# A four-layer graph network on one core: order of the prologue's loads, and where a scratch memory is cleared

## What is computed

```
edge_feat = concat([x[src], x[dst], edge_attr]); h = mish(edge_feat @ W1 + b1)
messages  = mish(h @ W2 + b2)
agg       = segment_sum(messages, dst)
u         = mish(concat([x, agg]) @ W3 + b3); y = x + u @ W4 + b4
x         = layernorm(x + (layernorm(y) * gamma + beta))
```

## Time and profile before

| | us |
|---|---|
| median of 3 runs | 1333.28 (1331.62 to 1339.01) |
| the profiled execution's own time | 1331.4 |
| its span | 1329.7 |
| PE busy in the span | 1249.7 (94%) |
| mean granted PE clock | 0.973 of full speed |
| start to last matmul of Z | 90.7 |
| first matmul of the edge phase | 96.9 |
| first matmul of block 1 | 110.9 |

### The profile page before, as it was taken

The page is one execution under the profiler, slowest core; times in us unless marked ns, Lnnn a source line. Parts: engine busy times, 40 slices in busy tenths (PEclk is TensorE's granted clock), DMA queues, the critical chain, the costliest instruction groups (busy, mean ns, idle before and its releaser), DMA issues. The chain is left out here.

```text
span 1329.7 us, 18809 instructions
## 1 busy us (share of the span) xinstructions
PE 1249.7 (94%) x5868; PEld 1000.0 (75%) x5868; DVE 1034.8 (78%) x1815; ACT 854.3 (64%) x775; POOL 665.9 (50%) x484
## 2 busy tenths in 40 slices
PE   6987999999999999999999999688799997999998
PEld 5766777777777777777777777467587775888886
DVE  3435999999999999999999999866776247847444
ACT  3307999999999999999999999437633011212210
POOL 0137688888878887888887886153230000011000
PEclk8998999999999999999999999889999997999999
DMA  9968777777777777777777777269200520000001
GB/s 308 329 213 175 155 148 153 155 152 157 152 148 146 151 156 153 153 154 156 157 151 144 148 157 175 57 231 348 99 2 0 202 66 15 17 1 2 1 20 59
DMA packets 105386, 178.34 MB, mean 134 GB/s; under 512 B 34786, under 2 KB 44304, under 8 KB 105320
## 3 DMA queue, kind: packets, MB, share of 16 engines
q0 software_dynamic: 71056, 106.45, 41.3%
q1 hardware_dynamic: 27176, 58.85, 12.8%
q10 hardware_dynamic: 7088, 12.20, 2.7%
HBM read 139.11 MB, written 38.15 MB: 133 GB/s over the span
## 5 line engine op out<-in xcount | busy, mean ns | idle before, releaser
L213 POOL DMA_INDIRECT w_raw<-q_dram,idx_all x172 | 332.8, 1935 | 73.3 <-issue 56.0
L932 PE MATMUL ps_x<-wA_hi,hT_hi 128*128 128x512 f32 x668 | 270.4, 405 | 1.3 <-DVE hT_lo L701 1.3
L932 PE MATMUL ps_x<-wA_hi,hT_lo 128*128 128x512 f32 x668 | 264.4, 396 | 0.0
L932 PE MATMUL ps_x<-wA_lo,hT_hi 128*128 128x512 f32 x668 | 264.1, 395 | 0.0
L213 POOL DMA_INDIRECT w_raw<-p_dram,idx_all x176 | 176.7, 1004 | 149.5 <-issue 106.3
L932 PEld LDWEIGHTS ps_x<-wA_hi,hT_hi 128*128 128x128 f32 x668 | 125.6, 188 | 34.1 <-issue 1.7
L932 PEld LDWEIGHTS ps_x<-wA_hi,hT_lo 128*128 128x128 f32 x668 | 125.5, 188 | 30.1
L932 PEld LDWEIGHTS ps_x<-wA_lo,hT_hi 128*128 128x128 f32 x668 | 125.5, 188 | 28.5
L708 DVE TENSOR_TENSOR x<-ps_x,b 128x512 f32<-128x512 f32 x167 | 113.7, 681 | 26.5 <-PE ps_x L932 24.4
L1602 POOL TENSOR_TENSOR tmp_n<-X,gam 128x512 f32<-128x512 f32 x10 | 13.9, 1393 | 225.6 <-DVE t_be L1687 180.8
L892 PE MATMUL ps_x<-ident,w_raw 128*128 128x128 f32 x672 | 103.4, 277 | 13.9 <-DVE h L694 7.6
(11 more groups left out here) (280 smaller groups left out, 2894.2 us busy)
## 6 DMA issues: line engine op xcount, KB each, us to landing
ea_raw<-in_eaT SPq DMA_DIRECT2D x88, 128.0 KB, 4.4
adj_dram<-adj_sb POOLq DMA_DIRECT2D x42, 210.2 KB, 9.7
adj_dram<-b ACTq DMA_DIRECT2D x11, 640.5 KB, 5.4
U_lo<-adj_dram SPq DMA_DIRECT2D x10, 640.0 KB, 8.1
adjT_dram<-adjT_sb SPq DMA_DIRECT2D x10, 640.0 KB, 7.4
w_raw<-in_w SPq DMA_DIRECT2D x5, 1024.0 KB, 8.1
adjT_rest<-adjT_dram SPq DMA_DIRECT2D x7, 640.0 KB, 9.9
w_raw_g<-in_w SPq DMA_DIRECT2D x4, 1024.0 KB, 7.7
```

The source lines that it names most:

```text
L213: g.indirect_dma_start(G[:, slot, c * D:(c + 1) * D], None, rows, bass.IndirectOffsetOnAxis(ap=idx_all[:, i:i + 1], axis=0), **op).then_in ...
L932: last = t.matmul(ps_x2[c % 2][:, :], h[:, b.slot, e], w[:, k, :], start=(k == 0 and i == 0), stop=(k == KD - 1 and i == 2))
```

## The change

In words, by engine:

- **ACT, loads:** `w0b` (1024 KB) is issued after the casts of `w0a` and of X1, no longer right behind `w0a`. Its casts move from tiles 1 to 4 to tiles 6 to 9 (DVE's matching subtractions too).
- **SP, loads:** W2 and `wc_raw` are issued behind the store of P0; the biases behind the store of P3; the first edge attributes behind the stores of Q0 and Q1.
- **ACT, clearing:** no pair stands in P. Pairs 0 to 3 alternate with the casts of W3; pair k waits until product R+2k+2 is out (`m_out`), and from pair 5 on the wait is `2R+1`, the first Z product. So pairs 5 to 10 are issued in one row from there.
- **SP, end:** Z's stores count on a semaphore that outlives the stage (`z0_out`). The stage's end no longer waits for their landing. `o_sb` shares memory with the edge phase's `x2` (its second half), so DVE waits for `z0_out` before it first writes there (block 1), and SP before it loads Z back in the first layer's stage.

```diff
-CLEAR_FROM = 1
+        z0_out = sem("z0_out")
+            x2 = sb("x2", [P, 2, TE * D], F32, edges)
-        o_sb = sb("o_sb", [P, OUTS, D], F32, ctx)
+        o_sb = x2[:, 1, :].rearrange("p (u d) -> p u d", u=OUTS)
...
-                sp.dma_start(w2_raw[:, :, :], by_slices(w02)).then_inc(w2_in, 16)
-                for half in range(2):
-                    sp.dma_start(wc_raw[half * ED:(half + 1) * ED, :], w0c).then_inc(w2_in, 16)
-                sp.dma_start(b1[:, :], bcast(b01)).then_inc(b_in, 16)
-                sp.dma_start(b2[:, :], bcast(b02)).then_inc(b2_in, 16)
-                sp.dma_start(b3[:, :], bcast(b03)).then_inc(b3_in, 16)
-                for b in range(2):
-                    load_edge_attr(sp, ea_raw, eaT, b, b, ea_in[b])
                 for r in range(R):
                     sp.wait_ge(p_evac, r + 1)
                     store(p_dram, r, r, st_out[r % OUTS])
+                    if r == 0:
+                        sp.dma_start(w2_raw[:, :, :], by_slices(w02)).then_inc(w2_in, 16)
+                        for half in range(2):
+                            sp.dma_start(wc_raw[half * ED:(half + 1) * ED, :], w0c).then_inc(w2_in, 16)
+                    if r == 3:
+                        sp.dma_start(b1[:, :], bcast(b01)).then_inc(b_in, 16)
+                        sp.dma_start(b2[:, :], bcast(b02)).then_inc(b2_in, 16)
+                        sp.dma_start(b3[:, :], bcast(b03)).then_inc(b3_in, 16)
...
                     store(q_dram, r, m, st_out[m % OUTS])
+                    if r < 2:
+                        load_edge_attr(sp, ea_raw, eaT, r, r, ea_in[r])
                 for r in range(ZM, R):
                     sp.wait_ge(z_evac, r - ZM + 1)
-                    store(z0_dram, r - ZM, 2 * R + r - ZM, z_out)
+                    store(z0_dram, r - ZM, 2 * R + r - ZM, z0_out)
...
-                sp.wait_ge(z_out, 16 * (R - ZM))
...
-                    if 2 <= r < 2 + KD:
-                        low(KD + r - 2)
+                    if r >= R - KD:
+                        low(2 * KD + r - R)
...
-                act.dma_start(w_raw[:, KD:, :], by_slices(w0b)).then_inc(w_in[KD], 16)
                 x_high(0)
                 for k in range(KD):
                     high(k)
-                act.wait_ge(z_ready, 1)
+                x_high(1)
+                act.dma_start(w_raw[:, KD:, :], by_slices(w0b)).then_inc(w_in[KD], 16)
                 for r in range(R):
...
-                    if 1 <= r < 1 + KD:
-                        high(KD + r - 1)
+                    if r >= R - KD:
+                        high(2 * KD + r - R)
...
-                    if r >= CLEAR_FROM:
-                        clear(r - CLEAR_FROM)
-                for r in range(R - CLEAR_FROM, DROWS // P):
-                    act.wait_ge(m_out, R + r - R + CLEAR_FROM + 1)
-                    act.sem_inc(turn, 1)
-                    clear(r)
+                act.wait_ge(z_ready, 1)
                 act.wait_ge(w3_in, 16)
                 act.wait_ge(m_out, R)
                 act.sem_inc(turn, 1)
                 for k in range(KD):
                     a.copy(w_hi[:, k, :], w2_raw[:, k, :]).then_inc(w3_hi, 1)
+                    act.wait_ge(m_out, R + 2 * k + 2)
+                    act.sem_inc(turn, 1)
+                    clear(k)
+                for r in range(KD, DROWS // P):
+                    act.wait_ge(m_out, min(R + 2 * r + 2, 2 * R + 1))
+                    act.sem_inc(turn, 1)
+                    clear(r)
...
+                        if c == 0 and b.it2 is None and b.k == 1:
+                            dve_.wait_ge(z0_out, 16 * (R - ZM))
                         dve_.wait_ge(x2_ready, b.count(TE, c + 1))
...
                     if s == 0:
+                        sp.wait_ge(z0_out, 16 * (R - ZM))
```

More of the change, by code:

```diff
@@ L192, in gnn @@
                     X, w_raw, b4, wA_hi, wA_lo, wc_hi, wc_lo, b2, b3, x, src, dst, w0a, w0b, w0c, b01, w02, b02, w03, b03,
-                    p_dram, q_dram, z0_dram, agg_dram, adj_dram, zero_out, p_in, q_in, eaT, ea_raw, ea_in)
+                    p_dram, q_dram, z0_dram, agg_dram, adj_dram, zero_out, p_in, q_in, eaT, ea_raw, ea_in, x2, z0_out)
             edge_phase(nc, sb, pb, sem, edge_sem, prep_sems, ident, half_pi, relT, srcT, qT, idx_all, base_f, base_i, npass, iota_src,
                        X, Y, w_raw, b3, b4, gam, bet, wA_hi, wA_lo, wc_hi, wc_lo, b2, p_dram, q_dram, agg_dram, adj_dram, eaT, w03,
-                       w04, b04, g0, be0, w3b_in, w4_in, vec_in, zero_out, p_in, q_in, ea_raw, ea_in)
+                       w04, b04, g0, be0, w3b_in, w4_in, vec_in, zero_out, p_in, q_in, ea_raw, ea_in, x2, z0_out)
         Y += [sb(f"Y{r}", [P, D]) for r in range(ZE, R)]
@@ L203, in gnn @@
         first_layer(nc, sb, pb, sem, edge_sems, ident, half_pi, eps_col, X, U_hi, U_lo, Y, w_raw, w_hi, w_lo, b3, b4, gam, bet, deg, rdeg, nrdeg, has, slow,
-                    agg_dram, adj_dram, adjT_dram, z0_dram, w1l, b1l, w1r, w3b_in, w4_in, vec_in, adjT_held, adj_held)
+                    agg_dram, adj_dram, adjT_dram, z0_dram, w1l, b1l, w1r, w3b_in, w4_in, vec_in, adjT_held, adj_held, z0_out)
         edge_numbers.close()
@@ L223, in prepare @@
             X, w_raw, zeros, w2_hi, w2_lo, wc_hi, wc_lo, b2, b3, x, src, dst, w0a, w0b, w0c, b01, w02, b02, w03, b03,
-            p_dram, q_dram, z0_dram, agg_dram, adj_dram, zero_out, p_in, q_in, eaT, ea_raw, ea_in):
+            p_dram, q_dram, z0_dram, agg_dram, adj_dram, zero_out, p_in, q_in, eaT, ea_raw, ea_in, x2, z0_out):
     with ExitStack() as ctx:
@@ L244, in prepare @@
         (z_ready, ident_ready, b_in, b2_in, b3_in, idx_in, pad_set, dve, w_hi_ready, w_lo_ready, idx_tr, idx_ready, t_ready, hi_ready,
-         lo_ready, m_out, p_evac, q_evac, z_evac, w2_in, w2_split, w2_low, w3_in, w3_hi, w3_lo, z_out, turn) = [
+         lo_ready, m_out, p_evac, q_evac, z_evac, w2_in, w2_split, w2_low, w3_in, w3_hi, w3_lo, turn) = [
             prep_sem("prep_" + n) for n in (
@@ L248, in prepare @@
                 "idx_ready", "t_ready", "hi_ready", "lo_ready", "m_out", "p_evac", "q_evac", "z_evac", "w2_in", "w2_split",
-                "w2_low", "w3_in", "w3_hi", "w3_lo", "z_out", "turn")]
+                "w2_low", "w3_in", "w3_hi", "w3_lo", "turn")]
         w_in = [prep_sem(f"prep_w_in{k}") for k in range(KD + 1)]
@@ L441, in _ @@
                     high(k)
-                act.wait_ge(z_ready, 1)
+                x_high(1)
+                act.dma_start(w_raw[:, KD:, :], by_slices(w0b)).then_inc(w_in[KD], 16)
                 for r in range(R):
-                    if r + 1 < R:
+                    if 1 <= r and r + 1 < R:
                         x_high(r + 1)
-                    if 1 <= r < 1 + KD:
-                        high(KD + r - 1)
+                    if r >= R - KD:
+                        high(2 * KD + r - R)
                     if 1 + KD <= r < 1 + 2 * KD:
@@ L524, in edge_phase @@
                X, Z, w_raw, b3, b4, gam, bet, w2_hi, w2_lo, wc_hi, wc_lo, b2, p_dram, q_dram, agg_dram, adj_dram, eaT, w03,
-               w04, b04, g0, be0, w3b_in, w4_in, vec_in, zero_out, p_in, q_in, ea_raw, ea_in):
+               w04, b04, g0, be0, w3b_in, w4_in, vec_in, zero_out, p_in, q_in, ea_raw, ea_in, x2, z0_out):
     HB = 2 * BE
@@ L538, in edge_phase @@
         hT_lo = sb("hT_lo", [P, 2, KD * BE], F32R, ctx)
-        x2 = sb("x2", [P, 2, TE * D], F32, ctx)
         m2 = sb("m2", [P, 2, TE * D], F32, ctx)
@@ L998, in first_layer @@
 def first_layer(nc, sb, pb, sem, sems_to_clear, ident, half_pi, eps_col, X, U_hi, U_lo, Z, w_raw, w_hi, w_lo, b3, b4, gam, bet, deg, rdeg, nrdeg, has, slow,
-                agg_dram, adj_dram, adjT_dram, z0_dram, w1l, b1l, w1r, w3b_in, w4_in, vec_in, adjT_held, adj_held):
+                agg_dram, adj_dram, adjT_dram, z0_dram, w1l, b1l, w1r, w3b_in, w4_in, vec_in, adjT_held, adj_held, z0_out):
     with ExitStack() as ctx:
```

## The result

The change makes the kernel slower: 1342.47 us (median of 19 runs, 1338.96 to 1344.72) against 1333.58 for the kernel before on the same chip, a ratio of 1.0062 with a 95% interval of [1.0051, 1.0073]. The forecast was 1335 with a range up to 1341, and the chance given to "slower by more than half a per cent" was 0.13. The span grew from 1329.7 to 1338.2 us, +8.5. Each profile shows one execution: 1339.84 us for the changed kernel and 1331.4 for the one before, 2 to 3 us under their medians.

What follows compares the result with a forecast made beforehand. PE was taken as the bound, with time to change only at four stops before 111 us. +2.9 at the stage's end, with P's -1.9 inside and 0 elsewhere, gave 1334.4 or 1336.3 us; forecast 1335, range 1326 to 1341.

Steps and rivals of the forecast that it cites:

- Loads in the order of use: At PE's wait for X2, 12.6 to 17.9 us: holding back `w0b` gains 0, X2 lands no earlier.
- The part of the 41-row loads: At PE's wait for X2: one DMA engine carries the 41-row index loads, and its 8 packets of X2 stand behind them.
- Rival C: At the start: X2 lands before 12.6 us, PE's wait and slow clock go, -7.7 us; 1327.5 in all, chance 0.15.
- SP's late loads: W2, biases and edge attributes, issued later, have 10 us and more until use; no cost counted.
- Product P, -1.9: From 23.7 to 53 us: PE's stops go, with no clearing store or `w0b` part left there, -1.9 us.
- the two stops: PE's stops in product P, 1.3 us at 40.4 us and a shorter one before; both were to go.
- Pairs 0 to 4 lie in Q and cost nothing; PE covers them: In Q: five pairs of clearing stores, one per 5.4 us, cost 0.
- ACT's row of issues: Behind Z's first product: pairs 5 to 10 issued in a row, held by a queue 110 packets ahead, ending at 97.8 us.
- What bounds the stage's end is ACT's issues: At the barrier after Z: ACT's issues replace SP's wait; first edge matmul at 99.8 instead of 96.9 us, +2.9.
- stop 3: PE idle from Z's last matmul to 96.9 us: SP waits 3.1 us for Z's stores, edge phase starts 2.0 us later.
- Block 1, 0 of 0 to +2.2: At block 1's start: its gathers beside queued clearing stores add between 0 and +2.2 us; 0 taken.
- Rival D: At the stage's end: ACT's queue holds less, some 60 packets per engine or fewer; 1340 to 1346 us, chance 0.13.

Runs made afterwards that it cites:

- 40-row kernels: The kernel before and the changed kernel, each with every 41-row index load cut into 40 rows and one row: 1327.06 and 1334.06 us.
- loads only: The kernel before with the change's new order of loads on SP, ACT and DVE, clearing stores and Z's stores as before: 1339.20 us, ratio 1.0040.
- Z only: The kernel before with only Z's stores outliving the stage, so SP no longer waits for them at its end: 1333.92 us, ratio 1.0006.

## Why the prediction was wrong

Step by step, in its own order.

- **Loads in the order of use, 0: right, with its reason.** X2's transposes start at 17.43 (17.89 before, and 16.5 to 18.2 in all kernels with 41-row loads). The part of the 41-row loads was confirmed by the 40-row kernels. Rival C's price, -7.7 us, is what the first of them measured at block 1 (-7.6). One figure of the step has no source: the earlier trace rows give 1.1 us until a load moves (0.9 to 2.0), not 1.9. In the changed kernel `w0b` was issued at 9.1 us, and ACT's queue moved its packets from 12.3 us on.
- **But the same step costed SP's late loads at nothing** ("have 10 us and more until use"). It asked when they are needed and not what they stand in front of. In loads only, where they stand beside the late `w0b`, the time is 5.4 us longer, through Q's stores. In the full change no such stop is seen; there the clearing stores had left P, which may be why.
- **Product P, -1.9: right in kind, too small.** Z's first product came 3.2 us earlier; 0.5 of it is X2, 1.9 the two stops, and the rest the shorter slow clock: 0.71 instead of 0.53 behind the stop.
- **"Pairs 0 to 4 lie in Q and cost nothing; PE covers them": wrong.** PE is covered, but POOL waits for Q's last store, which shares the engines with them. PE was 3.2 us ahead and the first gather 0.8 us late: 4 us lost.
- **ACT's row of issues: right in its number.** 98.4 against 97.8. Its queue held less than I took. Packets of ACT's queue from 50 to 98.4 us, and to 120 us, when all had moved:

```profile
q10 hardware_dynamic: 4595, 7.76, 46.5%
...
q10 hardware_dynamic: 5984, 10.10, 41.9%
```

  1389 packets, 87 per engine, were ahead when the last issue was done, not 110: 23 x 78 ns = 1.8 us more to wait for. The row began 1.3 us earlier than forecast, which made up for most of it. That the number came out is in part luck.
- **"What bounds the stage's end is ACT's issues", +2.9: this is the step that failed.** The sum had the gathers' 6.5 us of engine time in it, but as work that ACT's packets must pass, not as an end of its own. The gathers' own way, 10.9 us from the first start to the last landing before, grew to 17.0 beside the clearing stores. POOL leaves the stage behind its last gather, 101.3, and the edge phase starts 2.5 us later: 103.75 instead of 99.8. The forecast's own reading of stop 3, SP's wait for Z, was one of two nearly equal waits (POOL's DRAIN ends at 94.9 and SP's at 95.3), which Z only shows.
- **Block 1, 0 of 0 to +2.2: +0.6.** From the first edge matmul to block 1 it takes 14.6 us instead of 14.0. PE's matmuls ran at the lower of its two clocks (1.2 GHz) for longer: the fourth group of four transposes takes 0.91 us (at 109.34), where it took 0.60 (at 102.21) before.
- **Rival D** gave 1340 to 1346 and the measured time lies in it. Its mechanism was ACT held by a queue of 60 packets; the queue held 87 and ACT was on time. The sign was D's, the cause another.

Forecast against measured at block 1: +2.9 and +7.4. The missing 4.5 us are 3.9 at the stage's end and 0.6 behind it.

## What to carry to other kernels

Where the DMA engines are near full, an order of loads and stores is a plan for their time: what is taken out of a stretch in which PE hides it has to be moved in a later one, and here it delayed the gathers that the next stage waited for. So count, for each moved transfer, whose stores and gathers it now stands beside, not only when its data are used. When a wait at a barrier is removed, look for the second wait that ends within a microsecond of it. And before loads are reordered, look for a load whose number of rows has no large divisor up to 16, as 41 has none: splitting it brought 0.5% here, and no reordering brought anything.

## What the runs showed of the hardware

- POOL did not leave a stage before its indirect DMAs had landed, although the kernel's code has no wait for them there: POOL's DRAIN at the stage's end was over 0.54 to 0.55 us after the last landing in all twelve kernels that gather in the stage, and took 0.7 us in the two that don't. ACT's DRAIN took some 0.15 us while its clearing stores were still moving: plain stores on SP's and ACT's queues held no one.
- In the changed kernel ACT's queue was 87 packets per engine ahead at the end of its last issue, with stores of 640.5 and 256 KB alternating. The last two issues were held 4.45 and 2.48 us.
- A load of 41 rows cut into 40 and 1 was worth 6.7 us (0.5%) of a kernel of 1333 us, the stop and the slow clock behind it together.
